# The second layer's batch loop, its Vector, Tensor and Scalar orders rewritten: ranks at a batch's end, positions among the maxima

## What is computed

```python
xn = layernorm(x);  x = x + windowed_attention(xn) + quantized_linear(xn)     # layer one
xn = layernorm(x)                                                           # layer two
k, q, v = xn @ Wk.T + bk, xn @ Wq.T + bq, xn @ Wv.T + bv
attn = softmax(q @ k.T / n, axis=queries);   a = attn @ v / n
r = rms_norm(xn);  scores = r @ w_router.T;  w, idx = softmax(top2(scores)), top2 indices
for each token and each of its 2 experts:  (u, gate) = r @ w_up[e].T;  y = (u * silu(gate)) @ w_down[e].T
x = x + a + sum(w * y) + xn
```

## Time and profile before

| what | value |
|---|---|
| median of 3 runs (lowest to highest) | 561.87 us (557.76 to 562.17) |
| the profiled execution: its time, its span | 560.39 us, 558.6 us |
| PE, DVE, ACT, POOL busy over the span | 86%, 75%, 61%, 55% |
| load of one expert chunk (L1829), issue to landing | 2.2 us |
| one scatter DMA (L1298), issue to landing | 2.3 us |
| `rows_of` of a batch, scaling of two experts' weights, `gate_exp` on ScalarE | 1.9 us, 1.3 us, 0.2 us |
| store of `x1s`, load of `xall`, issue to landing (medians) | 2.5 us, 2.7 us |

### The profile page before, as it was taken

One profiled execution on the slowest core, in us unless ns is written; L12 is line 12 of the kernel. 1 busy time (PEld: TensorE's weight loads), 2 busy tenths in 40 slices (PEclk: granted clock), 3 DMA queues, 4 the chain that ended last, 5 costly groups with the idle time before them and its releaser, 6 DMA issues. The chain is left out here.

```text
span 558.6 us, 17265 instructions
## 1 busy us (share of the span) xinstructions
PE 482.9 (86%) x5963; PEld 321.7 (58%) x5963; DVE 417.6 (75%) x1508; ACT 341.4 (61%) x870; POOL 306.2 (55%) x361
## 2 busy tenths in 40 slices
PE   6288898898989988989889997988979799999991
PEld 5135344454444454544445455656666699999991
DVE  6688678778797787886886734899988767567762
ACT  2072687777777777777755775675555555555551
POOL 6680764634836746558201020557776777777673
PEclk9575899999999999999997999999979899999997
DMA  3866138076383471743820020811113333545552
GB/s 85 201 144 128 47 86 183 22 170 119 101 168 98 131 156 52 180 98 102 167 61 22 22 78 20 308 33 45 41 43 87 92 92 102 142 148 150 175 172 98
DMA packets 51381, 61.00 MB, mean 109 GB/s; under 512 B 10001, under 2 KB 42133, under 8 KB 49696
## 3 DMA queue, kind: packets, MB, share of 16 engines
q1 hardware_dynamic: 45824, 50.26, 37.0%
q0 software_dynamic: 4320, 8.47, 4.3%
q10 hardware_dynamic: 1152, 1.18, 0.7%
HBM read 31.68 MB, written 28.39 MB: 108 GB/s over the span
## 5 line engine op out<-in xcount | busy, mean ns | idle before, releaser
L721 DVE CUSTOM_DVE_ANT_0 A<-A,band 128x320 f32<-128x320 f32 x256 | 123.3, 498 | 28.0 <-PE A L904 27.9
L942 PE MATMUL SB<-Qs,Ks 50*64 50x320 bf16 (+2 forms) x1024 | 124.0, 294 | 3.6 <-ACT Pb L563 2.9
L904 PE MATMUL A<-Ks,Qs 48*64 48x320 bf16 (+2 forms) x1024 | 111.6, 301 | 17.2 <-DVE mneg L721 9.9
L566 ACT ACTIVATE Pb<-SB 128x320 f32<-128x320 f32 x256 | 96.4, 441 | 38.4 <-PE SB L956 36.8
L716 DVE TENSOR_REDUCE mneg<-A 128x2 f32<-128x384 f32 (+1 forms) x128 | 79.5, 621 | 27.5 <-PE A L912 27.3
L904 PEld LDWEIGHTS A<-Ks,Qs 48*64 48x64 bf16 x1024 | 46.7, 109 | 92.4 <-DVE mneg L721 39.9
L969 PE MATMUL PV<-Pb,Va 128*32 128x320 f32 (+2 forms) x1024 | 86.9, 412 | 5.5 <-ACT Pb L563 4.5
L563 ACT ACTIVATE Pb<-SB 128x384 f32<-128x384 f32 (+1 forms) x128 | 66.3, 545 | 39.4 <-PE SB L956 39.2
L1871 POOL DMA_INDIRECT results<-y,xt x71 | 74.9, 1055 | 28.1 <-issue 24.5
L1298 POOL DMA_INDIRECT expert_rows<-pay,pos x64 | 61.9, 967 | 50.7 <-DVE pay L1483 32.4
L956 PE MATMUL SB<-ends,ident 64*64 64x128 bf16 x768 | 83.8, 221 | 0.0
(11 more groups left out here) (273 smaller groups left out, 928.6 us busy)
## 6 DMA issues: line engine op xcount, KB each, us to landing
Qs<-parts_dram SPq DMA_DIRECT2D x14, 384.0 KB, 5.7
Ks<-parts_dram SPq DMA_DIRECT2D x14, 384.0 KB, 9.0
xt<-expert_rows SPq DMA_DIRECT2D x71, 65.0 KB, 2.2
yb<-results SPq DMA_DIRECT2D x7, 512.0 KB, 4.9
parts_dram<-qp SPq DMA_DIRECT2D x16, 192.0 KB, 2.9
parts_dram<-kp SPq DMA_DIRECT2D x14, 192.0 KB, 2.9
xb<-in_x SPq DMA_DIRECT2D x8, 256.0 KB, 3.1
parts_dram<-qp SPq DMA_DIRECT2D x16, 128.0 KB, 2.8
```

Source lines behind the costliest of these rows:

```text
L566: act.activation(Pb[:, group % 4, c, 0:w], bank[:, 0:w], ACT.Exp).then_inc(act_exp, 1)
L721: nc.vector.tensor_tensor_reduce(bank[:, 0:w], bank[:, 0:w], band[:, skip:skip + w], -1.0, 3e38, ALU.add, ALU.min, mneg[:, step % 2, first ...
L904: mm = nc.tensor.matmul(bank[out:out + HP, at:at + w], Qs[b % RING][rows, a, HP * sub:HP * sub + HP], Ks[b % RING][rows, a, lo:lo + w], st ...
L942: nc.tensor.matmul(out[r0:r0 + HP, at:at + w], Ks[b % RING][rows, a, HP * sub:HP * sub + HP], Qs[b % RING][rows, a, lo:lo + w], start=not ...
```

## The change

`NX` becomes 7: batch 6 is loaded, measured and rooted at the end of layer one, and batch 7 is loaded first thing in layer two, measured at the end of VectorE's batch 0 and rooted ahead of scatter 1.

`rank(g+1)` moves on TensorE from behind the scores of batch g+1 to directly behind the product of batch g; in batch 0 the scores go ahead of `turn(1)`. `route_b` becomes `place`: it starts a batch, and its pieces stand between the four maxima (in batch 0 ahead of them). `route_a` becomes `choose`: the pieces stand between the four rows of the norm (of the same batch as before), with `evac_v` behind the first piece. The reciprocals and the scalings are staggered by one or two. `gate_exp(g)` moves on ScalarE to the head of batch g. `early_tiles` moves behind `choose`, all but its first operation, and `rows_to_pad` behind `place`, and so behind the maxima.

```diff
@@ -51,7 +51,7 @@
...
 WARM_TAIL = 12
-NX = 6
+NX = 7
 FILLS = ((0, 7), (2,), (3,), (1, 6), (4,), (5,))
@@ -354,6 +354,7 @@
...
         sp.dma_start(base_r[:], base_dram[NB - 1]).then_inc(dma_base_r, 16)
+        load_x1(NB - 2)
         sp.wait_ge(dve_x1, NB)
@@ -835,6 +836,9 @@
...
                         ffn_out(g, u - 57)
+        for i in range(NT):
+            tail["moments"](NB - 2, i)
+        tail["stat"](NB - 2)
         context(NB - 1, 0, misc)
@@ -1250,9 +1254,6 @@
...
-        sp.wait_ge(dma_x, 16)
-        sp.dma_start(xall[:, NX + 1], xv[NX + 1]).then_inc(dma_x, 16)
         sp.wait_ge(dma_pad_hw, 16)
@@ -1306,8 +1307,8 @@
...
             for g in range(NB):
-                if 3 <= g < 3 + NB - NX:
-                    roots(NX + g - 3, mhalf)
+                if g == 1:
+                    roots(NX, mhalf)
                 scatter(g, g % 2)
@@ -1368,8 +1369,7 @@
...
                 p, last = g % 2, g == NB - 1
-                if last or g == 0:
-                    gate_exp(g)
+                gate_exp(g)
                 if not last:
@@ -1380,8 +1380,6 @@
...
                     evac_q(g + 1, 1 - p)
-                    if g > 0:
-                        gate_exp(g)
                     evac_k(g + 1, 1 - p)
@@ -1404,13 +1402,19 @@
...
-        def norm_of(g):
+        def norm_ready(g):
             dve.wait_ge(pool_roots, NROOT * g + 2)
...
+        def norm_row(g, i):
+            nc.vector.tensor_scalar(xn[g % 3][:, i, :], xall[:, g, i, :], mv[:, g, i, 0:1],
+                                    inv[:, 0, g, i:i + 1], ALU.subtract, ALU.mult).then_inc(dve_xn, 1)
+        def norm_of(g):
+            norm_ready(g)
             for i in range(NT):
-                nc.vector.tensor_scalar(xn[g % 3][:, i, :], xall[:, g, i, :], mv[:, g, i, 0:1],
-                                        inv[:, 0, g, i:i + 1], ALU.subtract, ALU.mult).then_inc(dve_xn, 1)
+                norm_row(g, i)
@@ -1444,43 +1448,83 @@
...
-        def ranks(g, last):
+        def choose(g, p):
+            ra, normed = RA * g, g + 1
+            dve.wait_ge(pe_v, g + 1)
+            dve.wait_ge(act_em, g)
+            dve.wait_ge(pool_roots, NROOT * (g + 1))
+            nc.vector.tensor_tensor(sc[:].rearrange("p (b i) e -> p b i e", b=2), blocks[:, :, :, P:P + NE],
+                                    inv[:, 1, g, :].rearrange("p (b i) -> p b i", b=2).unsqueeze(3)
+                                    .to_broadcast([P, 2, 2, NE]), ALU.mult).then_inc(dve_ra, 1)
+            evac_v(g, p)
+            dve.wait_ge(dve_ra, ra + 1)
+            for i in range(NT):
+                nc.vector.max(mx[:, i, :], sc[:, i, :]).then_inc(dve_ra, 1)
+            if normed < NB:
+                norm_ready(normed)
+                norm_row(normed, 0)
+            dve.wait_ge(dve_ra, ra + 1 + NT)
+            for i in range(NT):
+                nc.vector.max_index(ix[:, i, :], mx[:, i, :], sc[:, i, :]).then_inc(dve_ra, 1)
+            if normed < NB:
+                norm_row(normed, 1)
+            dve.wait_ge(dve_ra, ra + 1 + 2 * NT)
+            nc.vector.tensor_copy(ixf[:], ix[:]).then_inc(dve_ra, 1)
+            if normed < NB:
+                norm_row(normed, 2)
+            dve.wait_ge(dve_ra, ra + 2 + 2 * NT)
+            nc.vector.tensor_tensor(oh[p][:], iota8[:].unsqueeze(1).unsqueeze(1).to_broadcast([P, NT, TOPK, NE]),
+                                    ixf[:, :, 0:TOPK].unsqueeze(3).to_broadcast([P, NT, TOPK, NE]), ALU.is_equal)\
+                .then_inc(dve_ra, 1)
+            if normed < NB:
+                norm_row(normed, 3)
+            dve.wait_ge(dve_ra, ra + 3 + 2 * NT)
+            nc.vector.tensor_tensor(M[p][:], oh[p][:, :, 0, :], oh[p][:, :, 1, :], ALU.add).then_inc(dve_ra, 1)
+            nc.vector.tensor_tensor(dm[:], mx[:, :, 1], mx[:, :, 0], ALU.subtract).then_inc(dve_ra, 1)
+        def place(g, p, maximum):
+            rb = RB * g
+            order = (4, 4, 4, 4) if g == 0 else (0, 1, 2, 3)
+            def maxima_at(n):
+                for kt in range(NT):
+                    if order[kt] == n:
+                        maximum(kt)
             dve.wait_ge(pe_rank, g + 1)
-            if last:
+            if g == NB - 1:
                 dve.wait_ge(pe_cnt, 1)
-            if not (isinstance(g, int) and g == 0):
-                dve.wait_ge(dve_rb, RB * g)
+            if g > 0:
+                dve.wait_ge(dve_rb, rb)
             nc.vector.tensor_tensor(Re[:], RT[:, 0:NT * NE].rearrange("p (i e) -> p i e", e=NE),
...
-        def route_b(g, p):
...
+            dve.wait_ge(act_em, g + 1)
+            nc.vector.tensor_scalar(den[:], em[:], 1.0, None, ALU.add).then_inc(dve_rb, 1)
+            maxima_at(0)
+            dve.wait_ge(dve_rb, rb + 1)
+            nc.vector.tensor_tensor(prod[:], oh[p][:], Re[:].unsqueeze(2).to_broadcast([P, NT, TOPK, NE]), ALU.mult)\
+                .then_inc(dve_rb, 1)
+            nc.vector.tensor_reduce(msum[:], M[p][:].rearrange("p i e -> p e i"), AX.X, ALU.add).then_inc(dve_rb, 1)
+            nc.vector.tensor_scalar(dest[:], dest[:], float(TOPK * NT), None, ALU.add).then_inc(dve_rb, 1)
+            maxima_at(1)
+            dve.wait_ge(dve_rb, rb + 3)
+            nc.vector.tensor_reduce(posf[:], prod[:], AX.X, ALU.add).then_inc(dve_rb, 1)
             dve.wait_ge(act_pay2, g + 1)
-            done[0] = done[0] + 1
...
+            nc.vector.reciprocal(pay[p][:, 0, :, P], den[:]).then_inc(dve_rb, 1)
+            dve.wait_ge(dve_rb, rb + 4)
+            nc.vector.tensor_tensor(S[1 - p][:], S[p][:], msum[:], ALU.add).then_inc(dve_rb, 1)
+            maxima_at(2)
+            dve.wait_ge(dve_rb, rb + 6)
+            nc.vector.tensor_copy(pos[p][:], posf[:]).then_inc(dve_rb, 1)
+            nc.vector.tensor_copy(
                 pay[p][:, :, :, P + 1].bitcast(I32).rearrange("p k i -> p i k"),
-                dest[:].rearrange("p (i k) -> p i k", k=TOPK)))
-            step(nc.vector.reciprocal(pay[p][:, 0, :, P], den[:]))
-            step(nc.vector.tensor_tensor(pay[p][:, 1, :, P], em[:], pay[p][:, 0, :, P], ALU.mult), False)
+                dest[:].rearrange("p (i k) -> p i k", k=TOPK)).then_inc(dve_rb, 1)
+            dve.wait_ge(dve_rb, rb + 7)
+            nc.vector.tensor_tensor(pay[p][:, 1, :, P], em[:], pay[p][:, 0, :, P], ALU.mult).then_inc(dve_rb, 1)
+            maxima_at(3)
+            maxima_at(4)
@@ -1508,10 +1552,8 @@
...
-            evac_v(0, 0)
-            norm_of(1)
             dve.wait_ge(dve_const, 7)
-            route_a(0, 0)
+            choose(0, 0)
@@ -1544,11 +1586,15 @@
...
+        def rows_seen():
+            seen = RT[:, CNT + SEEN * NE:CNT + (SEEN + 1) * NE]
+            step(nc.vector.tensor_scalar(full_a[:], seen, 1.0 / P, -(P - 1) / (2 * P), ALU.mult, ALU.add), False)
...
-            seen = RT[:, CNT + SEEN * NE:CNT + (SEEN + 1) * NE]
             tiles = [1, EARLY, NE]
-            step(nc.vector.tensor_scalar(full_a[:], seen, 1.0 / P, -(P - 1) / (2 * P), ALU.mult, ALU.add))
+            dve.wait_ge(dve_fin, fin[0])
             step(nc.vector.tensor_scalar(full[:], full_a[:], MAGIC, MAGIC, ALU.add, ALU.subtract))
@@ -1600,45 +1646,49 @@
...
                 p, o, last = g % 2, 1 - g % 2, g == NB - 1
-                ranks_first = last or g == 0
...
+                def maximum(kt):
                     dve.wait_ge(pe_S, NT * g + kt + 1)
...
                         .then_inc(dve_max, 1)
-                if not ranks_first:
-                    ranks(g, last)
+                def share(kt):
+                    dve.wait_ge(act_exp, NT * g + kt + 1)
+                    nc.vector.reciprocal(srec[:, kt:kt + 1], ssum[:, kt:kt + 1]).then_inc(dve_rec, 1)
+                def weigh(kt):
+                    dve.wait_ge(dve_rec, NT * g + kt + 1)
+                    nc.vector.tensor_scalar(vs[:, kt, :], v[p][:, kt, :], srec[:, kt:kt + 1], ISC, ALU.mult, ALU.mult)\
+                        .then_inc(dve_vs, 1)
+                place(g, p, maximum)
+                if last:
+                    rows_to_pad()
                 if g == SEEN:
...
                 if g == SEEN + 1:
-                    early_tiles()
...
+                    rows_seen()
+                dve.wait_ge(pe_out, g)
+                dve.wait_ge(dve_v, g + 1)
+                share(0)
+                share(1)
+                weigh(0)
+                share(2)
+                weigh(1)
+                share(3)
+                weigh(2)
+                weigh(3)
                 if last:
...
                 else:
-                    if not ranks_first:
-                        route_b(g, p)
-                    evac_v(g + 1, o)
-                    if g + 2 < NB:
-                        norm_of(g + 2)
-                    route_a(g + 1, o)
+                    choose(g + 1, o)
+                if g == 0:
+                    for i in range(NT):
+                        moments(NX, i)
+                    stat(NX)
+                if g == SEEN + 1:
```

(20 more changed lines are left out.)

29 lines of the change are left out of this document (removed).

## The result

| | before | after |
|---|---|---|
| median (lowest to highest) | 559.82 us (554.92 to 562.17), 4 runs | 548.61 us (546.90 to 549.95), 4 runs |
| the profiled execution: time, span | 560.39, 558.6 us | 549.95, 548.2 us |
| ratio of the runs, 95% interval | | 0.985 (0.981 to 0.989) |

The change makes the kernel 1.5% faster (1.1 to 1.9% by the interval). First the eight products, in the timeline of TensorE after; they answer to the earlier trace rows.

A forecast was written before the change was run, and what follows sets the result against it. VectorE was taken to bound batches 2 to 6. A 10.4 us period, batch 0's +1.65 and the extras' 1.35 put product 7 6.4 us sooner: 560.4 - 6.4 = 554.0 us, range 549.5 to 560.

The forecast's parts named there:

- the relay: Layer-two loop: scores, maxima, exponentials, reciprocals and scalings, product follow one another; by itself this takes 10.16 us a batch.
- the period: Loop, product to product: 10.16 + 0.2 (ranks) + 0.25 (positions) - 0.2 (staggered scalings) = 10.4 us.
- The positions between the maxima: VectorE: pieces of place stand in the gaps between four maxima and delay the fourth by 0.25 us (bounds 0 and 0.8).
- The stagger: VectorE: fewer reciprocals and scalings follow the fourth exponential, so the product comes 0.2 us sooner (bounds 0 and -0.3).
- The choice under the product: VectorE: the choice, five waits shorter, takes 3.1 us and is ready 0.7 us before the ranks need it.
- Batch 0: Start of layer two: ScalarE's copy waits for a turning behind the scores, so product 0 comes 1.65 us later.
- The extras: VectorE, once each: order_constants charged 0.5 us where it waits for the fourth exponential, early_tiles behind the choice 0.85 us.
- The padding: Loop's end: padding stores start later, the ninth chunk is turned 15.6 us after product 7's start, and it still hides.
- The clock at product 7: TensorE: the clock, full to half in this product (5.47 us), is assumed still to fall; if it holds, -1.6 us.
- The waits that were to come back: First rival, VectorE: small operations still start 0.2 us apart; period 11.2 us, time 559.6 us; 14 in 100.
- The second rival: Loop: GpSimd's floor is reached at a period of 10.1 us and product 7's clock holds; 550.3 us; 16 in 100.
- The payload's ring: Third rival: den waits through gate_exp and rows_of for a scatter's landing; at 8.5 us landing, 566.6 us; 5 in 100.

The follow-up runs named there:

- e6: The changed kernel with reciprocals and scalings in pairs again, as before the change; one execution took 557.61 us.
- e4: The changed kernel with the norm's four rows together ahead of the choice's chain, so its steps wait for their neighbours; one execution took 551.55 us.
- e9: The changed kernel with 1, 2 and 3 spare VectorE additions ahead of the choices made in batches 1, 2 and 3; one execution took 551.14 us.
- e3: The changed kernel with turn(1) ahead of the scores of batch 0, as before; median 548.81 us of 4 runs, ratio to before 0.979.
- e10: The changed kernel with turn(1) ahead of batch 0's scores and order_constants moved into layer one; median 548.63 us of 6 runs, ratio to before 0.984.
- e5: The changed kernel with all operations of the positions ahead of the four maxima in every batch; one execution took 548.67 us.
- e11: The changed kernel with ranks behind the scores and positions behind the maxima in batches 1 to 6; median 550.86 us of 10 runs, ratio to before 0.987.
- e1: The kernel before, with early_tiles, all but its first operation, moved behind the next choice in batch 5; median 557.62 us of 10 runs, ratio 0.998.
- e7: The kernel before, with only batch 6 loaded and measured in layer one; median 555.25 us of 10 runs, ratio 0.996.

## Why the prediction was right, and where its sizes were off

The direction and the mechanism were right: VectorE, without a pause before, has pauses now, and the relay sets the period. The amount was not: 554.0 was forecast, the profiled execution took 549.95, and the median of 548.61 lies 0.9 below the range of 549.5 to 560. The span fell by 10.4 us and not by 6.4. By its parts:

| part | forecast | measured |
|---|---|---|
| layer one | 0 | -0.41 |
| first ranks to product 0 | +1.65 | +1.53 |
| product 0 to 7 | -8.08 | -10.38 |
| product 7 itself | 0 | -1.63 |
| from its end on | 0 | +0.49 |

One reading on the way to the mechanism was wrong, though not its conclusion. `route_a` of batch 1 does lie between product 0 and batch 1's maxima; only `route_b` is absent there. What sets batch 1 apart is that VectorE waits in it, which the prediction did not show:

```profile
358.81 0.16 DVE L1445 TENSOR_TENSOR dm<-mx 128x4 f32<-128x4 f32 x1
359.49 0.69 DVE L1643 TENSOR_TENSOR x2b<-l_OU,l_xn 128x512 f32<-128x512 f32 x1 [0.52 <-PE l_OU L1741]
360.71 0.69 DVE L1613 TENSOR_REDUCE l_mneg<-l_S 128x1 f32<-128x512 f32 x1 [0.54 <-PE l_S L1726]
```

**The step that was mis-sized is the period**, 10.4 us for 10.12: seven times 0.28 is 2.0 us. The ranks cost 0.19 (0.2 was taken). The positions between the maxima cost 0.07, not 0.25. Their three pieces took 0.32, 0.26 and 0.26 us (383.17 - 382.25 - 0.60, and so on), 0.84 in all. I had taken 1.02, for ten operations. One of the ten, `den`, stands ahead of the first maximum, and for the other nine I had removed too little for the waits. 0.78 was free, so nearly the whole term was the error in the pieces. The stagger gave 0.29, close to the bound that I had set (0.3), and I took 0.2; e6 shows it by itself (0.33 in batch 3).

**The choice under the product** held: ready 0.79 us early against 0.7, and e4 and e9 show the price of its waits (0.11 to 0.18 us, not 0.12 each) and its margin. **Batch 0** held, and e3 shows its cause. ScalarE's copy waits for a turning behind the scores, and TensorE stands idle for it:

```profile
352.12 0.60 PE L1707 MATMUL l_XR<-l_ident,l_xn 128*128 128x128 f32 x4
353.41 1.12 PE L1744 MATMUL l_QK<-l_xnT,l_wqk 128*128 128x512 f32 x2 [0.69 <-ACT l_xnT L1320]
```

**The extras** took 1.13 us (0.53 and 0.6), not 1.35. **The padding** hid, as forecast (turned at +13.9 and not +15.6, as product 7 was 1.6 shorter). **Product 5** ran at the full clock, as the sum assumed.

**The clock at product 7** was kept at a loss, by the nearer row, and held. That was luck, good or bad: no argument of the prediction decided it. With 2.18 to 2.31 us of idle time ahead of it, product 7 held in three profiles (after, e9, e10) and fell in four (e3, e4, e5, e11). The two levels (2.4 and 1.2 GHz), with the same 2.19 us ahead: the stretch of product 7 after, and in e4 (busy PE, PEld, DVE, ACT, POOL, clock, DMA share, GB/s; for e4 PE alone).

```profile
428.50:432.40 3.90, 3.89 (x34) 3.89 (x35) 3.56 (x13) 2.77 (x5) 2.98 (x4) 1.00 0.36 105
```

```profile
428.60:434.10 5.50, 5.47 (x34) 0.69 0.38 111
```

So 1.6 us of the profiled gain is not the change's for certain. What is its own, up to product 7's start, is 8.85 us (80.05 from the first ranks, before 88.90). Part of it is product 5, which took 6.73 us before and 3.84 now. What decides between the two levels at the same idle time stays open.

**The rivals.** The waits that were to come back did not: the smallest operations started 0.07 us apart, and the period was 10.12. The Trainium skill, page "VectorE: DVE Perf Modes", section "The DRAIN you can't avoid", reports eight copies for which a semaphore after each cost nothing extra. In the small operations here it does: the four waits on the operation just before cost 0.11 to 0.18 us each in e4. But e5 shows that the positions could have stayed together: what their order needed was another operation between a result and its use.

The second rival's number, 550.3, came nearest to the profiled execution. Its size came true, its cause did not: the period of 10.12 is the relay's own sum (4.30 + 3.71 + 2.12), and the chain that ended last has no piece on GpSimd. That GpSimd's floor is 10.1 us too is a coincidence as far as these traces show. But it leaves no room: a relay much faster than that would have met it next.

The payload's ring, the third rival, did not bind: ScalarE never waited for a scatter to land. It was the kernel before that had this wait (18.3 us, with no DMA in the chain that ended last), and in e1 it reached TensorE.

## What to carry to other kernels

Where an engine's order has no pauses, count its waits on the operation just before; an independent operation in between took 0.11 to 0.18 us off each here, and it mattered little which one. Fit pieces into a rhythm by their measured start distances: an error of 0.28 us in a loop body was 2 us here. When a forecast rival's number comes true, ask the chain of work whether its cause did. And compare executions stage by stage from a common mark: a single execution that looked 9 us slower (e6) had lost 2.5 to its edit up to product 7.

## What was not expected of the hardware

- TensorE's clock: with 2.2 us of idle time ahead of product 7 it fell in four executions and held in three; elsewhere it held once with 2.89 and fell with 2.82 and 2.94. In the five products with 3.0 us and more ahead of them it fell each time. Three us in two parts with 2.05 us of work between did not lower it (e7); 1.22 and 0.82 with 1.12 between did (e1).
- The first ranks stood at 344.2 to 353.0 us in 14 profiles, though only the last 20 us or so ahead of them differed among the kernels.
- A fall can move rather than go: taken from product 5 in e1, it came one batch later and made a projection take twice its time. In e7 and after it did not.
- The same pair of scalings on VectorE took 0.46 us or up to 0.72, by where it fell behind the start of a scatter's DMA on GpSimd.
